# Reordering DVE's, ACT's and PE's lists in the tail of the routed linear stage

## The reference

```python
def _L1_ffn_ref(x, W_base, b_base, W_router, A, B):
    ...
    logits = x_flat @ W_router.T
    probs = jax.nn.softmax(logits, axis=-1)
    topk_probs, topk_idx = jax.lax.top_k(probs, TOP_K)
    topk_probs = topk_probs / jnp.sum(topk_probs, axis=-1, keepdims=True)
    onehot = jax.nn.one_hot(topk_idx, NUM_EXPERTS, dtype=x.dtype)
    combine = jnp.einsum('nk,nke->ne', topk_probs, onehot)
    h = jnp.einsum('nd,erd->ner', x_flat, A)
    hw = h * combine[:, :, None]
    expert_out = jnp.einsum('ner,eor->no', hw, B) * SCALING
    base_out = x_flat @ W_base.T + b_base
    out = base_out + expert_out
...
    x = x + _L1_attn_a_ref(_layernorm(x, axis=-1), ...)
    x = x + _L1_ffn_ref(_layernorm(x, axis=-1), ...)
    x = x + _L1_attn_b_ref(_layernorm(x, axis=-1), ...)
    x = x + _L1_ffn_ref(_layernorm(x, axis=-1), ...)
```

## Time and profile before

| | before |
|---|---|
| median of 3 runs | 2234.33 us (2233.85 to 2237.15) |
| the profiled execution, its own time | 2229.33 us |
| its span, first to last instruction | 2227.5 us |
| PE busy | 2059.9 us (92%) |
| DVE busy | 1392.1 us (62%) |
| ACT busy | 1162.9 us (52%) |
| POOL busy | 830.8 us (37%) |
| mean granted clock of PE | 0.962 of full speed |

### The profile page before, as it was taken

The page is one execution under the profiler, slowest core; times in us unless marked ns, Lnnn a source line. Parts: engine busy times, 40 slices in busy tenths (PEclk is TensorE's granted clock), DMA queues, the critical chain, the costliest instruction groups (busy, mean ns, idle before and its releaser), DMA issues. The chain is left out here.

```text
span 2227.5 us, 33255 instructions
## 1 busy us (share of the span) xinstructions
PE 2059.9 (92%) x11536; PEld 1471.6 (66%) x11536; DVE 1392.1 (62%) x2509; ACT 1162.9 (52%) x2691; POOL 830.8 (37%) x1011
## 2 busy tenths in 40 slices
PE   5999987998999999999987789999999987999988
PEld 3333345787888888888865657777777665744457
DVE  5888564635666666666655646666666556767756
ACT  4677643236556566566543545555555533335553
POOL 0000100225455455456340145545554421747611
PEclk8999978999999999999998989999999998989999
DMA  3000013580121121111011254344333210743301
GB/s 119 1 1 1 1 46 110 162 272 12 47 67 39 48 67 39 48 58 48 29 39 41 84 126 104 87 114 114 88 92 74 67 60 30 208 91 72 72 25 39
DMA packets 95732, 158.10 MB, mean 71 GB/s; under 512 B 12063, under 2 KB 33567, under 8 KB 93390
## 3 DMA queue, kind: packets, MB, share of 16 engines
q1 hardware_dynamic: 85774, 134.19, 21.2%
q0 software_dynamic: 9792, 21.77, 4.1%
HBM read 90.91 MB, written 31.46 MB: 55 GB/s over the span
## 5 line engine op out<-in xcount | busy, mean ns | idle before, releaser
L2570 POOL TENSOR_TENSOR attn1a_probs<-attn1a_probs,attn1a_recip 128x128 f32<-128x128 f32 (+3 forms) x256 | 178.9, 720 | 233.2 <-DVE attn1a_recip L2753 232.6
L1920 POOL TENSOR_TENSOR attn0b_probs<-attn0b_probs,attn0b_recip 128x128 f32<-128x128 f32 (+3 forms) x256 | 196.1, 787 | 184.6 <-DVE attn0b_recip L2164 184.5
L2624 ACT ACTIVATE attn1a_probs<-attn1a_scores,attn1a_negmax 128x128 f32<-128x128 f32 (+3 forms) x256 | 132.7, 523 | 173.5 <-DVE attn1a_negmax L2739 172.2
L2024 ACT ACTIVATE attn0b_probs<-attn0b_scores,attn0b_negmax 128x128 f32<-128x128 f32 (+3 forms) x256 | 132.7, 524 | 121.9 <-DVE attn0b_negmax L2157 121.3
L1471 DVE TENSOR_REDUCE attn0a_negmax<-attn0a_by_query 128x2 f32<-128x1024 f32 x128 | 151.8, 1218 | 10.3 <-PE attn0a_by_query L1588 10.3
L2739 DVE TENSOR_REDUCE attn1a_negmax<-attn1a_scores 128x2 f32<-128x256 f32 (+3 forms) x128 | 105.4, 823 | 70.3 <-PE attn1a_scores L2944 70.2
L1913 POOL TENSOR_TENSOR attn0b_q_cos<-attn0b_q_cos,attn0b_q_swap 128x512 f32<-128x512 f32 x64 | 84.2, 1316 | 160.0 <-DVE attn0b_q_swap L2146 160.0
L2032 ACT ACTIVATE attn0b_probsT_hi<-attn0b_turned 128x256 fp32r<-128x256 f32 (+3 forms) x128 | 90.1, 704 | 88.3 <-PE attn0b_turned L2308 86.7
L2157 DVE TENSOR_REDUCE attn0b_negmax<-attn0b_scores 128x2 f32<-128x256 f32 (+3 forms) x128 | 104.9, 820 | 46.6 <-PE attn0b_scores L2297 46.6
L2956 PE MATMUL attn1a_turned<-ident_f,attn1a_probs 128*128 128x128 f32 x640 | 116.8, 281 | 8.6 <-DVE attn1a_probsT L2747 6.4
L2143 DVE TENSOR_TENSOR attn0b_q_cos<-attn0b_aux,attn0b_cos_q 128x512 f32<-128x512 f32 x60 | 41.5, 691 | 116.3 <-ACT attn0b_q_swap L2045 116.3
(11 more groups left out here) (539 smaller groups left out, 6199.5 us busy)
## 6 DMA issues: line engine op xcount, KB each, us to landing
pre<-in_b_o SPq DMA_DIRECT2D x16, 1024.0 KB, 5.5
attn1a_qT<-attn1a_stage SPq DMA_DIRECT2D x128, 128.0 KB, 3.1
attn1a_qT<-attn1a_stage SPq DMA_DIRECT2D x64, 256.0 KB, 3.9
attn0b_vals<-attn0b_v_out SPq DMA_DIRECT2D x16, 512.0 KB, 3.7
attn0b_keys<-attn0b_part SPq DMA_DIRECT2D x32, 256.0 KB, 3.9
pre<-in_b_q SPq DMA_DIRECT2D x8, 1024.0 KB, 7.4
attn0b_kT<-attn0b_keys SPq DMA_DIRECT2D x64, 128.0 KB, 2.8
pre<-in_b_kv SPq DMA_DIRECT2D x5, 1024.0 KB, 6.3
```

The lines of the kernel that those rows point to most:

```text
L1920: pool.tensor_tensor(x, x, recip[:, r % DEEP, e:e + 1].broadcast_to([P, (qt + 1) * P]), ALU.mult).then_inc(s_scaled, 1)
L2024: act.activation(probs[:, r % DEEP, e, 0:width], scores[r % 2][:, e, 0:width], ACT.Exp, bias=negmax[:, r % 2, e:e + 1], accum_out=sums[:, ...
L2570: pool.tensor_tensor(x, x, recip[:, r % DEEP, e:e + 1].broadcast_to([P, (qt + 1) * P]), ALU.mult).then_inc(s_scaled, 1)
L2624: act.activation(probs[:, r % DEEP, e, 0:width], scores[r % 2][:, e, 0:width], ACT.Exp, bias=negmax[:, r % 2, e:e + 1], accum_out=sums[:, ...
```

## The change

DVE's list in the tail is rewritten: `share(1)` moves in front of `add(1)`, `add(2)` in front of `weighted_lo(1)`, and behind `add(3)` every turn is `lo(t)`, `factors(t + 2)`, `add(t + 4)`. On ACT the roots leave the pair with `normalise` and are issued a place earlier: `root(t + 3)` stands in front of `hi(t)`, and `normalise(t + 2)` behind it. On PE each of `turn(0)` to `turn(3)` stands in front of one `experts` of the second half. No instruction is added or removed; in the last stage only DVE's list changes, since the `second` parts do not exist there.

```diff
@@ ACT
-            if not project:
-                scaled(second, 0)
-                scaled(second, 1)
-            weighted_hi(1)
-            if not project:
+            if project:
+                weighted_hi(1)
+            else:
+                second.root(act, m, 0)
+                second.root(act, m, 1)
+                second.normalise(act, m, 0)
+                weighted_hi(1)
+                second.root(act, m, 2)
+                second.normalise(act, m, 1)
                 for t in range(TILES):
+                    if t + 3 < TILES:
+                        second.root(act, m, t + 3)
                     second.hi(act, t, final(m.xnT_hi, t))
                     if t + 2 < TILES:
-                        scaled(second, t + 2)
+                        second.normalise(act, m, t + 2)
@@ DVE
             add_base(7)
             add(0)
+            share(1)
             add(1)
-            share(1)
             factors(0)
+            add(2)
+            weighted_lo(1)
             factors(1)
-            weighted_lo(1)
-            add(2)
             add(3)
-            second_lo(0)
-            factors(2)
-            second_lo(1)
-            factors(3)
-            add(4)
-            second_lo(2)
-            add(5)
-            factors(4)
-            second_lo(3)
-            add(6)
-            factors(5)
-            second_lo(4)
-            factors(6)
-            second_lo(5)
-            add(7)
-            factors(7)
-            second_lo(6)
-            second_lo(7)
+            for t in range(TILES):
+                second_lo(t)
+                if t + 2 < TILES:
+                    factors(t + 2)
+                if t + 4 < TILES:
+                    add(t + 4)
@@ PE
             turn_weighted(1)
-            if not project:
-                second.turn(pe, m, 0)
-                second.turn(pe, m, 1)
             for t in range(HALF, TILES):
+                if not project:
+                    second.turn(pe, m, t - HALF)
                 experts(t)
-                if not project and 5 <= t < 7:
-                    second.turn(pe, m, t - 3)
```

## The result

| | before | changed |
|---|---|---|
| median, first comparison (10 runs each) | 2233.45 us | 2228.10 us |
| lowest and highest of these | 2229.71 to 2237.15 | 2223.18 to 2232.09 |
| ratio, 95% interval | | 0.9979 (0.9969 to 0.9989) |
| the profiled execution: time, span | 2229.33, 2227.5 us | 2228.90, 2227.2 us |

The changed kernel is 0.2% faster, 4.7 us by the ratio (2233.45 x 0.0021). The two profiled spans differ by 0.3 us only, because the changed kernel's execution came into the first routed tail 2.3 us later (`add(0)` at 1855.32 instead of 1853.05), took about 1 us longer in the attention stage behind it, and 1.2 us longer from the last add to the end of the span (5.2 against 4.1).

A forecast was written before the change was run, and what follows sets the result against it. No engine was taken as the bound of the first routed tail, but the chain over PE, DVE and ACT. First tail 2.7 plus last stage 0.5 gave 3.2 us less than 2234.33: 2231.1 us, range 2228.8 to 2235.2.

The forecast's parts named there:

- The front of the tail: DVE in the first routed tail, up to `add(3)`: it starts at 1860.78 instead of 1863.35, winning 2.6 us.
- The new turn: DVE's turn in the first routed tail: 3.34 us, 0.92 of it waiting behind the root; `lo(3)` level with before.
- What follows `lo(4)`: End of the first routed tail: `add(7)` is already done, so `turn(7)` comes at 1880.77 instead of 1883.39, 2.6 us sooner.
- PE's clock: End of PE's work in the first routed stage: 2.7 us less taken, between 1.1 and 4.2 depending on clock levels.
- The last stage: Last routed stage: `share(1)` and PE's turned half 0.6 us earlier, the end 0.5 us earlier, bounds 0 and 0.6.
- Both terms at their best: First tail 4.2 us and last stage 0.6 us, together 4.8 us less, 2229.5 us; chance 20%.
- The low level through all projections: First routed tail: PE at low clock becomes the bound, loss up to 1.3 us, 2235.6 us; 8% for the mechanism.
- A wait of 1.3 us a turn: First routed tail: the roots' wait is 1.3 us instead of 0.92, leaving 0.8 us of gain, 2233.0 us; 15%.
- ACT could pass it: First routed tail: ACT not held by the root, turns of 2.42 us, stage ends 7 us sooner, 2226.8 us; 2%.

The follow-up runs named there:

- hi_first: The changed kernel with `hi(t)` in front of `root(t + 3)` on ACT instead of behind it; 2222.44 us, ratio 0.9957 to the kernel before.
- add7_early: The kernel before with only `add(7)` moved, from behind `lo(5)` to behind `factors(5)`; 2228.33 us, ratio 0.9979 to the kernel before.
- old_pe: The changed kernel with PE's list as in the kernel before; 2229.25 us, ratio 0.9983 to the kernel before.
- before_3: The kernel before, unchanged, timed once more as a control; 2234.53 us, ratio 1.0011 to the kernel before.

## Why the prediction came out as it did

**The front of the tail** was right: `add(1)` starts 3.49 us behind `add(0)` (expected 3.49), `add(3)` 7.67 behind it (expected 7.73).

**The new turn** was right in size and in cause. I had 3.34 us, of which 0.92 lost to the root in front of `hi`; the trace has 3.35, of which DVE's profile shows 0.84 as idle. `lo(3)` stands 20.21 us behind `add(0)`, expected 20.21, before 20.33: level, as said. hi_first showed the cause by removing it.

**What follows `lo(4)`** was right: `turn(7)` at 27.75 (expected 27.72), and the end at 29.81 in the first trace (expected 29.79 with the high level). add7_early showed that the place of `add(7)` is most of the gain of the first tail: 1.9 of 2.6 us level against level, and on the mean of the traces all of it. PE's order brings nothing that old_pe could show; the look-ahead of the other tiles and the moved roots were not timed each by itself.

**PE's clock** was the term of uncertain size, 2.7 us for the tail within 1.1 and 4.2. The mean of the traces gives 2.8. The reason that I gave, that the idle in front of the last turns is gone, agrees with the traces: the last `turn` and projection ran high in all three of the changed kernel. What I left out of the 2.7 was that the low level also falls on the first two projections, where it now costs 1.1 to 1.2 us in two traces of three. That what the clock costs before (0.94) and after (0.75) nearly cancels, and so leaves my 2.7 almost as it was, is luck.

**The last stage** was right: 0.6 at the turned half, 0.5 at the end.

**What failed is the step from the sum to the time and the range.** The likeliest time, 2231.1, was 3.0 us too high: the median of before was 0.9 lower beside the changed kernel than my 2234.33, and the medians lie 5.35 apart where my sum had 3.2. I wrote that the runs' own scatter is 3.3 us between lowest and highest, and hung the forecast on the median of those three runs, 2234.33. Over 124 runs the same kernel goes from 2226.09 to 2241.25 us, with a mean of 2232.0. Three runs said little of this: against that mean the base was 2.3 us too high, and the range, which ended 0.7 us under my best case, had no room for comparisons that by themselves lie 2 us apart. Against the ratio, 3.2 us less (0.9986) lies inside the interval of the first comparison; the pooled 4.2 plus or minus 1.1 also holds it, barely. The traces show 2.8 + 0.5 = 3.3 us. Whether the change gives another 0.9 us elsewhere, or whether this is scatter, is not settled; a share in the next stage's clock is possible, since before_3 lost 1.4 us there and no trace of the changed kernel did, but one trace does not give its size.

**The rivals.** "Both terms at their best", 4.8 us, is nearest to the first comparison, but not for its reason: the tail's mean gain is 2.8, not 4.2. The low level through all projections did not come up in full. A wait of 1.3 us a turn, which was to leave nothing of the gain, did not come: DVE idled 0.84 to 0.85. That the root costs nothing, or that ACT could pass it, is refuted by hi_first. The sum of that last rival kept one wait too many: three turns of 2.42 behind a `lo(0)` without its wait of 0.92 put `lo(3)` at 1869.6 and not at 1870.5, and hi_first has it 16.40 us behind `add(0)`, which is 1869.45 on the clock of the trace before; its tail ended 9.0 us sooner than that trace's, not 7.

## What to carry to other kernels

When a list is made to run further ahead, follow what each engine's queue then holds: a root issued early for a later tile stood in front of work that was ready and took 0.9 us of every turn, and swapping two lines gave another 5 us. Ask of each moved line alone what it brings to the end; here one `add` out of the way of the last tile's chain brought as much, within what the runs can tell, as the whole rewritten list. And before a range is set on a change of a few us, find out how far two runs of the same kernel lie apart.

## What the runs showed of the hardware

- Runs of one kernel on one core, over all groups, scatter by 15 us (2226.09 to 2241.25), and the mean granted clock goes with it: the kernel before had spans of 2226.9, 2227.5 and 2235.2 us at 0.965, 0.962 and 0.960 in the profiles, and over the 114 runs of it whose clock was noted a mean of 2226.2 us at 0.965 and 2234.1 at 0.960. In a tail of 30 us the moments of the low level alone move the end by 1.2 to 1.6 us from run to run with the same instructions.
- Most of that scatter arises where no list was changed. In the fourteen traces `add(0)` of the first tail starts between 1852.3 and 1861.7 us, the stretch from the next stage's first product to the last stage's `add(0)` takes 323.2 to 328.0, and that from the last add to the end of the span 3.9 to 6.0. A gain of a few us is seen in its own stretch long before it is seen in the run time.
- Extra products of 512 columns in PE's idle times, 21 to 42 of them a tail, cost the tail nothing (ends of 32.41, 29.81, 29.82 and 24.98 us). The kernel before and the changed one were about 3 us faster with them; hi_first was not clearly so (0.9959 against 0.9957).
